# Homes of the split operands by high and low part, and a new order of their products, in an adaLN + bit-FFN kernel

## The reference

```python
ada = (timestep_embed @ ada_w + ada_b)[:, None, :]
shift1, scale1, gate1, shift2, scale2, gate2 = jnp.split(ada, 6, axis=-1)
x1 = _ln(x) * (1.0 + scale1) + shift1
qkv = (x1 @ qkv_w + qkv_b).reshape(Bc, Tc, 3, H, DH)      # 16 heads of 128
attn = softmax(einsum('bthd,bshd->bhts', q, k) * scale)
attn_out = einsum('bhts,bshd->bthd', attn, v).reshape(Bc, Tc, INNER) @ out_w + out_b
x = x + gate1 * attn_out
x2 = _ln(x) * (1.0 + scale2) + shift2
x = x + gate2 * (gelu(x2 @ ffn_w1 + ffn_b1) @ ffn_w2 + ffn_b2)
...
def _linear_bit(x, w, g):          # 8-bit rows, ternary weights
    return einsum('bsd,od->bso', _act_quant(_rmsnorm(x, g)), _ternary_quant(w))
h = silu(_linear_bit(x, w1, g1)) * _linear_bit(x, w2, g2)
return x_in + _linear_bit(h, w3, g3)
```

## Time and profile before

| | us |
|---|---|
| median of 3 runs | 314.59 |
| range of the 3 runs | 314.19 to 314.69 |
| the profiled execution, device time | 313.21 |
| its span (first to last instruction) | 311.4 |
| PE busy / PEld busy | 303.4 / 271.1 |
| DVE / ACT / POOL busy | 220.0 / 187.3 / 122.9 |

### The profile page before, as it was taken

One profiled execution on the slowest core, in us unless ns is written; L12 is line 12 of the kernel. 1 busy time (PEld: TensorE's weight loads), 2 busy tenths in 40 slices (PEclk: granted clock), 3 DMA queues, 4 the chain that ended last, 5 costly groups with the idle time before them and its releaser, 6 DMA issues.

```text
span 311.4 us, 9815 instructions
## 1 busy us (share of the span) xinstructions
PE 303.4 (97%) x4171; PEld 271.1 (87%) x4171; DVE 220.0 (71%) x451; ACT 187.3 (60%) x358; POOL 122.9 (39%) x109
## 2 busy tenths in 40 slices
PE   8999999999999999999999999999999999999986
PEld 5887989999898989989899998789997789998664
DVE  3675885878286585972578058879277887996996
ACT  2765484638424674476546836587555677468793
POOL 2366502200732592598020621257330254223590
PEclk9999999999999999999999999999999999999999
DMA  7789836050053545112020010200010200200002
GB/s 238 262 236 268 275 103 246 2 159 14 2 134 73 172 105 172 51 48 73 3 71 2 2 36 2 68 2 2 30 40 2 69 4 2 69 1 2 0 34 71
DMA packets 21171, 24.49 MB, mean 79 GB/s; under 512 B 2020, under 2 KB 18696, under 8 KB 21128
## 3 DMA queue, kind: packets, MB, share of 16 engines
q1 hardware_dynamic: 20752, 23.57, 24.9%
q10 hardware_dynamic: 376, 0.30, 0.3%
HBM read 22.74 MB, written 1.11 MB: 77 GB/s over the span
## 4 chain that ended last, share of the span: by engine, by line
PE 91%; DVE 3%; ACT 2%; issue 2%; DMA 1%; POOL 0%; ACTq 0%; DVEq 0%; POOLq 0%
PE proj_banks L598 43%; PE out_bank L598 15%; PE wide_banks L598 5%; PE turn_bank L598 5%; PE proj_banks L669 4%; PE att_banks L700 4%; PE wide_banks L899 2%; PE att_banks L598 2%; PE wide_banks L700 1%; PE att_banks L933 1%; ACT work L2015 1%; DMA xin<-in_x 1%; PE att_banks L899 1%; PE wide_banks L783 1%; PE proj_banks L899 1%
## 5 line engine op out<-in xcount | busy, mean ns | idle before, releaser
L1872 ACT ACTIVATE q_t<-proj_banks,bias_cols 128x256 f32<-128x256 f32 x64 | 30.3, 474 | 47.1 <-PE proj_banks L598 46.4
L598 PE MATMUL proj_banks<-x_hi,w_hi 128*128 128x256 f32 x252 | 51.6, 286 | 0.0
L598 PE MATMUL proj_banks<-x_hi,w_lo 128*128 128x256 f32 x252 | 49.6, 278 | 0.0
L598 PE MATMUL proj_banks<-x_lo,w_hi 128*128 128x256 f32 x252 | 49.5, 278 | 0.0
L598 PEld LDWEIGHTS proj_banks<-x_hi,w_hi 128*128 128x128 f32 x252 | 39.1, 188 | 2.6 <-issue 1.1
L598 PEld LDWEIGHTS proj_banks<-x_hi,w_lo 128*128 128x128 f32 x252 | 38.2, 188 | 0.0
L598 PEld LDWEIGHTS proj_banks<-x_lo,w_hi 128*128 128x128 f32 x252 | 38.2, 188 | 0.0
L1371 DVE STREAM_TRANSPOSE att_banks<-att_banks 128x512 f32<-128x512 f32 x16 | 11.7, 728 | 33.7 <-PE wide_banks L700 32.5
L1872 ACT ACTIVATE k_t<-proj_banks,bias_cols 128x256 f32<-128x256 f32 x64 | 30.0, 469 | 0.0
L1339 DVE TENSOR_TENSOR v_sb<-proj_banks,bv_row 128x512 f32<-128x512 f32 x32 | 21.5, 686 | 5.4 <-issue 3.2
L598 PE MATMUL proj_banks<-w_hi,x_hi 128*128 128x512 f32 x64 | 21.2, 413 | 0.0
(11 more groups left out here) (329 smaller groups left out, 769.5 us busy)
## 6 DMA issues: line engine op xcount, KB each, us to landing
stage<-in_L_cond_qkv_w SPq DMA_DIRECT2D x16, 256.0 KB, 4.0
gate<-gate_rows_scratch SPq DMA_DIRECT2D x48, 64.0 KB, 2.3
stage<-in_L_cond_qkv_w SPq DMA_DIRECT2D x4, 512.0 KB, 4.7
stage<-in_L_cond_out_w SPq DMA_DIRECT2D x16, 128.0 KB, 4.1
work<-in_L_ffn_w SPq DMA_DIRECT2D x2, 1024.0 KB, 6.5
xin<-in_x SPq DMA_DIRECT2D x7, 256.0 KB, 3.4
bv_row<-in_L_cond_qkv_b SPq DMA_DIRECT2D x4, 256.0 KB, 6.4
work<-in_L_cond_ada_w SPq DMA_DIRECT2D x1, 1024.0 KB, 8.1
```

The costliest lines, as they stand in the source:

```text
L598: mm = pe.matmul(dst, l, r, start=start and i == 0, stop=stop and i == len(seq) - 1)
L1872: act.activation(dst[:, h, :], head_bank(u, h)[:, s * QT:(s + 1) * QT], ACT.Identity, bias=bias_cols[:, c:c + 1]).then_inc(qk_kept, 1)
```

## The change

It does three things.

1. **Homes.** Class by high and low part: `x1_hi`, all `w_lo`, `wo_lo`, `f1_lo`, `f2_lo`, `q_t`, `at_hi`, `stage` (with `h_hi`) are of class 0; `x1_lo`, `w_hi`, `wo_hi`, `f1_hi`, `f2_hi`, `k_t`, `v_sb`, `at_lo` and `h_lo` of class 64.
2. **Order.** Two new helpers stand beside `three_pass`. `weight_rows` (q/k and FFN 1) does for each pair low-high, high-high, high-low (stationary named first). `token_rows` (v, output projection, FFN 2) does all high-high first and then, pair by pair, high-low and low-high. `three_pass` stays for the first head of a quarter (`late` of `x1_lo`), for the first v half of units 0, 1, 8 and 9, and for the first tile of each `ffn1`.
3. **Waits.** `qk_lo` is waited for before the first matmul of a head instead of the fifth; `at_lo_made` before the 6th matmul of `out_proj` instead of the 9th; `h_lo_made` in `ffn2` pair by pair before the 10th, 14th, 18th and 22nd matmul instead of all of them before the 17th; in `late_ffn2` and `end_ffn2` before the 4th of six instead of the 5th.

```diff
         x1_hi = sb("x1_hi", [P, NQ, KD, QT], F32R)
-        x1_lo = sb("x1_lo", [P, NQ, KD, QT], F32R)
-        f2_hi = sb("f2_hi", [P, MT, D], F32R)
...
+        w_lo = [sb(f"w_lo{s}", [P, WO], F32R) for s in range(2)]
+        wo_lo = [sb(f"wo_lo{s}", [P, HG, D], F32R) for s in range(2)]
+        f1_lo = sb("f1_lo", [P, KD, MLP], F32R)
+        f2_lo = sb("f2_lo", [P, MT, D], F32R)
+        q_t = sb("q_t", [P, HG, QT])
+        at_hi = sb("at_hi", [P, 2, HG, P], F32R)
+        stage = sb("stage", [P, WO + HG * D])
+        floor.start(STEP)
+        x1_lo = sb("x1_lo", [P, NQ, KD, QT], F32R)
         w_hi = [sb(f"w_hi{s}", [P, WO], F32R) for s in range(2)]
+        wo_hi = [sb(f"wo_hi{s}", [P, HG, D], F32R) for s in range(2)]
         f1_hi = sb("f1_hi", [P, KD, MLP], F32R)
+        f2_hi = sb("f2_hi", [P, MT, D], F32R)
+        k_t = sb("k_t", [P, HG, QT])
...
-        h_lo = at("h_lo", [P, MT, QT], F32R, floor.where["stage"] + 4 * MT * QT)
+        h_lo = at("h_lo", [P, MT, QT], F32R, floor.where["stage"] + 4 * MT * QT + STEP)
...
+            def weight_rows(dst, pairs):
+                seq = [p for a, b, c, d in pairs for p in ((b, c), (a, c), (a, d))]
+                for i, (l, r) in enumerate(seq):
+                    mm = pe.matmul(dst, l, r, start=i == 0, stop=i == len(seq) - 1)
+                return mm
+
+            def token_rows(dst, pairs, start=True, stop=True, low={}, each=None):
+                seq = [(a, c) for a, b, c, d in pairs] + [p for a, b, c, d in pairs for p in ((a, d), (b, c))]
+                for i, (l, r) in enumerate(seq):
+                    if each is not None and i < len(pairs) and i % 2 == 0:
+                        pe.wait_ge(each[0], each[1] + i // 2 + 1)
+                    if i - len(pairs) - 1 in low:
+                        made, n = low[i - len(pairs) - 1]
+                        pe.wait_ge(made, n)
+                    mm = pe.matmul(dst, l, r, start=start and i == 0, stop=stop and i == len(seq) - 1)
+                return mm
...
                     pe.wait_ge(qk_hi, HALVES * g + c + 1)
-                    if late is None:
-                        late = ("lhsT", (qk_lo, HALVES * g + c + 1))
-                    else:
-                        pe.wait_ge(qk_lo, HALVES * g + c + 1)
+                    pe.wait_ge(qk_lo, HALVES * g + c + 1)
...
+                if t == 0 and u % HALF < 2:
+                    mm = three_pass(v_bank(u, t), pairs, late=("rhs", (vw_lo, g + 1)))
+                else:
+                    mm = token_rows(v_bank(u, t), pairs)
...
-                three_pass(out_bank[:, t * D:(t + 1) * D],
+                token_rows(out_bank[:, t * D:(t + 1) * D],
...
-                           late=("lhsT", (at_lo_made, 2 * u + 2)) if t == 0 else None).then_inc(out_mm, 1)
+                           low={0: (at_lo_made, 2 * u + 2)} if t == 0 else {}).then_inc(out_mm, 1)
...
-                           late=("lhsT", *lows) if t == 0 else None,
+                           low={4 * j: (h_lo_made, (MT // 2) * b + j + 1) for j in range(MT // 2)} if t == 0 else {},
```

More of the change, by code:

```diff
@@ L620, in qk_unit @@
                             for k in range(KD)]
-                    mm = three_pass(head_bank(u, h)[:, s * QT:(s + 1) * QT],
-                                    [(hi[:, cols[k]], lo[:, cols[k]], x1_hi[:, Q, k, :], x1_lo[:, Q, k, :])
-                                     for k in range(KD)], late=late if s == 0 else None)
+                    dst = head_bank(u, h)[:, s * QT:(s + 1) * QT]
+                    pairs = [(hi[:, cols[k]], lo[:, cols[k]], x1_hi[:, Q, k, :], x1_lo[:, Q, k, :]) for k in range(KD)]
+                    if late is not None and s == 0:
+                        mm = three_pass(dst, pairs, late=late)
+                    else:
+                        mm = weight_rows(dst, pairs)
                 mm.then_inc(projected, 1)
@@ L655, in v_unit @@
                 cols = [slice(SLOT + k * GC, SLOT + (k + 1) * GC) for k in range(KD)]
-                three_pass(v_bank(u, t),
-                           [(x1_hi[:, Q, k, tok], x1_lo[:, Q, k, tok], w_hi[g % 2][:, cols[k]], w_lo[g % 2][:, cols[k]])
-                            for k in range(KD)], late=("rhs", (vw_lo, g + 1)) if t == 0 else None).then_inc(projected, 1)
+                pairs = [(x1_hi[:, Q, k, tok], x1_lo[:, Q, k, tok], w_hi[g % 2][:, cols[k]], w_lo[g % 2][:, cols[k]])
+                         for k in range(KD)]
+                if t == 0 and u % HALF < 2:
+                    mm = three_pass(v_bank(u, t), pairs, late=("rhs", (vw_lo, g + 1)))
+                else:
+                    mm = token_rows(v_bank(u, t), pairs)
+                mm.then_inc(projected, 1)
             def score(u):
@@ L816, in ffn1 @@
                     cols = slice(m * P, (m + 1) * P)
-                    mm = three_pass(banks[pair % 2][:, (m % 2) * QT:(m % 2 + 1) * QT],
-                                    [(f1_hi[:, k, cols], f1_lo[:, k, cols], x1_hi[:, b, k, :], x1_lo[:, b, k, :])
-                                     for k in range(KD)],
-                                    late=("rhs", (x2_lo_made, b + (2 if end else 1))) if m == 0 else None)
+                    dst = banks[pair % 2][:, (m % 2) * QT:(m % 2 + 1) * QT]
+                    pairs = [(f1_hi[:, k, cols], f1_lo[:, k, cols], x1_hi[:, b, k, :], x1_lo[:, b, k, :]) for k in range(KD)]
+                    if m == 0:
+                        mm = three_pass(dst, pairs, late=("rhs", (x2_lo_made, b + (2 if end else 1))))
+                    else:
+                        mm = weight_rows(dst, pairs)
                     if m % 2 == 1:
@@ L846, in late_ffn2 @@
                 last = j == MT // 2 - 1
[L847 removed]
+                mm = token_rows(proj_bank[0][:, t * D:(t + 1) * D],
                                 [(h_hi[:, m, tok], h_lo[:, m, tok], f2_hi[:, m, :], f2_lo[:, m, :])
                                  for m in (2 * j, 2 * j + 1)], start=(j == 0 and t == 0), stop=last and t == 1,
[L850 removed]
+                                low={0: low})
                 if last:
@@ L862, in end_ffn2 @@
                 tok = slice(t * P, (t + 1) * P)
-                mm = three_pass(end_rows[t], [(h_hi[:, m, tok], h_lo[:, m, tok], f2_hi[:, m, :], f2_lo[:, m, :])
+                mm = token_rows(end_rows[t], [(h_hi[:, m, tok], h_lo[:, m, tok], f2_hi[:, m, :], f2_lo[:, m, :])
                                               for m in (2 * j, 2 * j + 1)], start=(j == 0), stop=(j == last),
-                                late=("lhsT", (h_lo_dve, 2 + j + 1)) if t == 0 else None)
+                                low={0: (h_lo_dve, 2 + j + 1)} if t == 0 else {})
                 if j == last:
```

18 lines of the change are left out of this document (1 added, 17 removed).

## The result

| | us |
|---|---|
| changed kernel, median of 6 runs (range) | 316.61 (315.90 to 317.05) |
| kernel before beside it, median (range) | 314.03 (312.88 to 314.69) |
| ratio, 95% interval | 1.0088 [1.0057, 1.0119] |
| profiled execution of the changed kernel, and its span | 316.38, 314.6 |

A forecast was written before the change was run, and what follows sets the result against it. TensorE's own pace on the split matmuls was taken to bound the kernel (PE busy 97%). Terms -0.70 - 0.3 + 0.2 - 0.3 + 0.2 = -0.9 us, off the median 314.59, gave 313.7 us; range 311.0 to 317.4.

The forecast's parts named there:

- The toggling inside bursts: Split-matmul bursts, operands now changing class each matmul: paces stay as they are, 0 us (bounds -2.7 and +4.1).
- the toggling disturbs each matmul: Rival, chance 0.25: every class change of the streamed operand slows the steps, bursts never settle; 318.9 us, half of it 316.7.
- Borders out of v: Twelve borders from v to 256-column bursts: equal classes cause the high pace, different ones end it; -0.70 us.
- Borders from score to v: Ten borders from score's k_t to x1_hi, both class 0 before: v projections get shorter, -0.3 us (bounds 0 and -0.9).
- New borders of equal class: Some 40 new equal-class borders inside bursts that keep three_pass: +0.2 us (bounds 0 and 0.4).
- The wait for h_lo: FFN 2, first and second quarter: last part waited for later, when it is there; -0.3 us together.
- The wait for at_lo: Unit 15's output projection, sixth matmul: its weight load waits and lies bare, +0.2 us (bounds 0.1 and 0.3).
- The wait for qk_lo: Unit 1's head starts later: +0.45 us on PE, costing nothing because a later wait for the bias row's transfer covers it.
- All low: Rival, chance 0.18: new homes end the high pace in all bursts; 311.5 us, or 311.0 with v at 226 ns.
- Homes are worth nothing: Rival, chance 0.19: paces come from the moment a burst starts, not addresses; waits leave -0.1, 314.5 us.

The follow-up runs named there:

- first pattern kernel: Bare bursts of 24 fp32r matmuls, only byte offsets (streamed, loaded) differing, none of the reference's work; constant (0, 64) 113.4 or 117.8 ns a step, constant (0, 0) 120.0.
- the second one: Bare bursts varying the length of the matmul ahead, swapped classes, odd matmuls; constant streamed 0, loaded 64: 113.3 ns in 13 of 16, 117.8 in 3; swapped 117.7 to 117.8.
- The kernels with other small homes: Only small fp32 matmuls' operands moved (q_t, v_sb to class 0; k_t, probs_t to 64), in the kernel before and with the new order and waits: ratios 1.0028 and 1.0026.
- the order kernel: The change's new order and waits with the homes of before, against the kernel before: 313.09 against 313.42 us, ratio 0.9975; once more 313.13 against 312.91, ratio 1.0009.

## Why the prediction was wrong, point by point

**The toggling inside bursts** is the step that failed. I put it at 0, since "each pair differs, as before", with bounds of -2.7 and +4.1 us. It measured +4.2 over the 256-column steps and their count, 1,474 x 2.62 ns = +3.9 by the pace alone: nearly the whole upper bound. The reason given was wrong in itself. I had taken for granted that a matmul is fast when the tile it streams and the one loaded beside it differ; the first pattern kernel shows no low burst unless both classes also stay the same from one matmul to the next (0 of 16 with either changing), and the second one none with the two swapped. The rival "the toggling disturbs each matmul" had the mechanism and the price of the 256-column part (+4.1). Its +0.4 for v was too much: v rose by 1.1 ns a step instead of 2.5, and its longer steps fell by as much. It came to 318.9 (its own terms, with -0.1 for the waits, add up to 319.0) against 316.6 measured; the span rose by 3.1, the medians, before's own being 0.56 under the one that I had started from, by 2.6.

**Borders out of v**, -0.70: wrong sign, as far as it could be tested. Rows 3 show four matmuls at 117 behind v and then steps of 113; I read the border as what disturbs, and the low pace as what comes by itself. The runs show the reverse: behind a v of any other classes a burst is at 118 from its first steps on, and the disturbance at the old border is what lets it fall. In the changed kernel it couldn't show, since no burst falls that toggles; with v's weights alone moved, which changes the classes inside v too, the span was 1.5 us longer.

**Borders from score to v**, -0.3: not seen. The v projection with 24 low-paced matmuls behind (5.70 in the earlier trace rows) has no counterpart any more, and the 512-column steps as a whole moved by -0.06. The kernels with other small homes test it alone, since there `k_t` no longer is of the class of `x1_hi`: the ten v projections behind `score` took 28.68 us together instead of 28.80, and 28.74 instead of 28.75 with the order. That is -0.1 us at most.

**New borders of equal class**, +0.2: not seen apart from the toggling. The homes alone have 743 of them, half as many changes of the streamed class, and a mean step of 118.28 against 117.79; constant equal classes took 120.0 in the pattern kernel. So they do cost something; what the 45 of the changed kernel cost by themselves no run shows.

**The wait for h_lo**, -0.3: right. The steps at the wait in the second quarter went from 204 + 221 to two of about 118, -0.19, and the first quarter's one of 207 is gone, -0.09.

**The wait for at_lo**, +0.2: right, at the place and of the size put.

**The wait for qk_lo**, 0 by its cover: half right. From the end of the piece ahead to the end of this head the chain took 2.87 us before, 3.32 in the order kernel, +0.45 as put, and 3.42 in the changed one, where the slower pace comes on top. The cover was a transfer, and it isn't fixed: `v_sb` started at 29.12 before, 29.45 in the changed kernel, and 28.60 in the order kernel. The chain of the changed kernel, and under it that of the order kernel:

```profile
27.08 1.41 PE proj_banks L596 x6
28.49 0.96 issue
29.45 0.70 DVE v_sb L1358
```

```profile
26.90 1.40 PE proj_banks L596 x6
28.30 1.40 PE proj_banks L613 x6
29.70 0.69 PE proj_banks L688 x52
```

In the second PE doesn't wait at all, so that in such an execution the cover doesn't hide all of the 0.45; how much of it then counts no run shows. One profile shows one draw of such a cover.

**The rivals.** "All low" fell with the first run that had homes alone. "Homes are worth nothing" fell too, and with it the rule of the Trainium skill's page "TensorE: Matmul & The Clock Gate" (Part 2: What happens when you issue a matmul), that loading the next tile's weights takes no bandwidth from the running matmul: the same instructions on the same tile take 113.4 or 120.0 ns by the offsets alone. By that rule all patterns would have had one step. The measurement decides.

**Before stays the best.** The order and waits with the old homes are at 0.9975 [0.9950, 1.0] and 1.0009 [0.9990, 1.0028]: no gain that two measurements agree on. What the waits gave back, -0.28, is about what `at_lo` and the start of unit 1 took, +0.2 and up to +0.45.

**Still open** is what picks the pace of a burst of constant classes behind a bare weight load, and what sets the place in its cycle at which v ends. Neither the length of the matmul ahead, in 16 values, nor the class at the entry told it; the same entry gives both in the same run.

## What to carry to other kernels

For fp32r matmuls of 256 columns with a weight load each, keep the offset of each operand (modulo 128 bytes) constant through a burst, the loaded one at 64 and the streamed one at 0, and don't let either alternate, not even so that each neighbouring pair differs. That makes the low pace possible, not certain, and for 512 columns the same pair was the slowest. Before a disturbance is removed, look at the steps on both sides of it: here the disturbed border was the way down to the low pace, and the kernels without it lost where I had booked a gain. And a term that no row of the trace shows is not 0 because a plausible reason says so; a pattern kernel of 150 us would have measured it.

## What the runs showed that I had not expected

- An fp32r matmul of 256 columns with its weight load has a locked step when both offsets are constant: 113.4 or 117.8 ns with loaded 64 and streamed 0, 117.8 with loaded 0 and streamed 64, 120.0 with both at 0. So which of the two is at 64 matters as well.
- The patterns of toggling have cycles of their own, of which each step belongs to one kind of matmul: 114, 118, 122 in `weight_rows`, in the kernel and in the pattern alike.
- At 512 columns it is another order: constant equal classes 226.6 (or about 230), (0, 64) 228.4 to 229.0 as the cycle 226, 229, 232 (in some bursts of the kernel before 233.3), (64, 0) 233.8, the highest, though (64, 0) has the lowest step at 256 columns.
- One matmul with another class, in the midst of a burst, can move all that follow by 4.4 ns each, up or down. Behind twelve 512-column matmuls of (0, 64) the pace went down in 6 of 6.
